# Routed experts in 47 blocks of 128 rows of one expert, in place of 40 blocks of two 64-row halves

## The reference

```python
# per token row t of the 8 * 128 = 1024 rows (hidden size 256)
scores = softmax(t @ gate_w.T)                 # 16 experts
top 4 experts of the row, weights scaled
routed = sum over the 4: w * (silu(g) * u) @ w2[e].T,  g, u = split(t @ w13[e].T)   # 176 wide
shared = sigmoid(t @ sgate_w.T) * ((silu(t @ Sg) * (t @ Su)) @ Sd)                  # 704 wide
out = x2 + routed + shared
```

## Time and profile before

| | |
|---|---|
| three runs | 398.63, 402.02, 402.61 us, median 402.02 |
| the profiled execution | 403.16 us, of which the span from the first to the last instruction is 401.3 us |
| busy in the span | PE 344.7 us (86%), DVE 227.7, ACT 207.2, POOL 178.8 |
| mean granted TensorE clock | 0.933 of full |
| moved by DMA | 72.54 MB, 181 GB/s over the span |

### The profile page before, as it was taken

One profiled execution on the slowest core, in us unless ns is written; L12 is line 12 of the kernel. 1 busy time (PEld: TensorE's weight loads), 2 busy tenths in 40 slices (PEclk: granted clock), 3 DMA queues, 4 the chain that ended last, 5 costly groups with the idle time before them and its releaser, 6 DMA issues.

```text
span 401.3 us, 7934 instructions
## 1 busy us (share of the span) xinstructions
PE 344.7 (86%) x2362; PEld 217.5 (54%) x2378; DVE 227.7 (57%) x688; ACT 207.2 (52%) x557; POOL 178.8 (45%) x212
## 2 busy tenths in 40 slices
PE   6988899999999978789996697897796888789893
PEld 2446576766777755477774343443443444346672
DVE  3387689889896899533725233333243333343884
ACT  1265688788897568344331354454344444552221
POOL 5481315343360516670664344655465455443000
PEclk9899899999999999758996599999899899999998
DMA  7997995979889452120682325554454455452931
GB/s 222 302 282 223 426 278 154 275 224 274 224 222 271 130 159 80 43 109 29 254 331 72 116 86 155 159 154 154 125 182 138 144 159 154 136 164 91 361 111 53
DMA packets 41747, 72.54 MB, mean 181 GB/s; under 512 B 5346, under 2 KB 29042, under 8 KB 40562
## 3 DMA queue, kind: packets, MB, share of 16 engines
q1 hardware_dynamic: 35490, 56.08, 46.5%
q0 software_dynamic: 5376, 15.13, 11.2%
q10 hardware_dynamic: 848, 0.92, 0.9%
HBM read 40.58 MB, written 31.53 MB: 180 GB/s over the span
## 4 chain that ended last, share of the span: by engine, by line
PE 40%; DVE 20%; issue 13%; ACT 10%; another core or an unknown queue 7%; POOL 5%; DMA 4%; ACTq 0%; DVEq 0%; POOLq 0%; SPq 0%
PE bank L1719 10%; ACT probs L656 6%; PE bank L1459 6%; PE bank L1741 5%; DVE neg_max L917 5%; PE bank L1731 3%; DVE probs_t L923 2%; PE bank L1381 2%; PE bank L1373 2%; PE bank L1429 2%; PE bank L1402 2%; PE bank L1604 1%; POOL y_picks L603 1%; PE bank L1709 1%
## 5 line engine op out<-in xcount | busy, mean ns | idle before, releaser
L1719 PE MATMUL bank<-w,xbt 128*64 x160 | 58.0, 489 | 20.4 <-ACT xbt L787 15.5
L656 ACT ACTIVATE probs<-bank,neg_max 128x128 f32<-128x128 f32 x256 | 69.9, 416 | 6.2 <-DVE neg_max L917 5.1
L603 POOL DMA_INDIRECT y_picks<-yb,ids x40 | 39.3, 982 | 51.9 <-DVE yb L1265 44.7
L1721 PE MATMUL bank<-w_odd,xbt 128*64 128x352 f32 x160 | 58.1, 489 | 0.0
L1258 DVE TENSOR_TENSOR hb<-sg,bank 128x176 f32<-128x176 f32 x40 | 13.5, 338 | 71.5 <-ACT sg L795 29.3
L611 POOL DMA_INDIRECT xb<-x_slots,rows x40 | 38.5, 962 | 21.8 <-DVE ids L1274 8.7
L1719 PEld LDWEIGHTS bank<-w,xbt 128*64 128x64 f32 x160 | 21.8, 144 | 44.6 <-issue 37.5
L795 ACT ACTIVATE sg<-bank 128x176 f32<-128x176 f32 x40 | 12.7, 317 | 63.8 <-PE bank L1721 43.0
L543 POOL DMA_INDIRECT x_slots<-x,slots x32 | 32.3, 1009 | 27.5 <-DVE slots L1046 19.5
L917 DVE TENSOR_REDUCE neg_max<-bank 128x4 f32<-128x512 f32 x64 | 41.5, 683 | 5.3 <-PE bank L1373 4.6
L1743 PE MATMUL bank<-w_odd,hbt 128*64 128x256 f32 x160 | 43.8, 398 | 0.0
(11 more groups left out here) (181 smaller groups left out, 740.5 us busy)
## 6 DMA issues: line engine op xcount, KB each, us to landing
x_slots<-zero_b SPq DMA_DIRECT2D x16, 1072.0 KB, 11.1
w_odd<-w_in_dram SPq DMA_DIRECT2D x40, 256.0 KB
w<-w_in_dram SPq DMA_DIRECT2D x4, 1408.0 KB, 12.0
w<-w_in_dram SPq DMA_DIRECT2D x4, 1024.0 KB
yg<-y_picks SPq DMA_DIRECT2D x8, 512.0 KB, 7.0
ktc<-keys_d SPq DMA_DIRECT2D x16, 192.0 KB
sw_raw<-shared_in_dram SPq DMA_DIRECT2D x6, 384.0 KB, 3.4
keys_d<-ctxt_h SPq DMA_DIRECT2D x4, 512.0 KB, 6.8
```

Of the source, the lines that this page charges most:

```text
L603: pool.indirect_dma_start(y_picks[:, :], bass.IndirectOffsetOnAxis(ids[:, n:n + 1], 0), yb[:, n % RB, :], None).then_inc(yb_placed[n % RB] ...
L656: ins = act.activation(probs[:, g, j, :], ps_s[g][:, 128 * j:128 * j + 128], ACT.Exp, bias=neg_max[:, g, j:j + 1])
L1719: pe.matmul(ps_gu[n % 2][0:ROWS, 0:GU], xbt[:, n % 2, k, 0:ROWS], w13[:, bass.ds(experts[n], 1), k, :].rearrange("p e n -> p (e n)"), star ...
L1721: ins = pe.matmul(ps_gu[n % 2][ROWS:128, 0:GU], xbt[:, n % 2, k, ROWS:128], w13_odd[:, n % 2, k, :], start=k == 0, stop=k == KC - 1)
```

## The change

The block is now 128 rows of one expert. With that bound there can be 47 blocks: (4096 + 16 * 127) // 128. One up weight and one down weight serve the whole block, so `copy_up`, `w13_odd` and `w2_odd` go, and so does the load of all down weights ahead; SP brings each block's down weights (`load_down`) and, as the rows of a block are adjacent in `x_slots`, its rows too (`load_rows`), each behind a register load. POOL keeps `place_rows` only. AHEAD = 2: the up product of chunks 6 and 7 and their element-wise steps stand ahead of the blocks. TensorE loads its packed words one at a time, seven of the eight inside the loop; ACT loads none.

```diff
-ROWS = 64
-NBLK = -(-((B * T * TOPK + NE * (ROWS - 1)) // ROWS) // 2)
-RW = 3
+NBLK = (B * T * TOPK + NE * 127) // 128
+AHEAD = 2
...
-        w13_odd = place("w13_odd", [128, 2, KC, GU])
-        w2_odd = place("w2_odd", [128, RW, KC, D])
-        w2 = place("w2", [128, NE, KC, D])
+        w2 = place("w2", [128, RB, KC, D])
...
+            def load_rows(n):
+                if n >= RB:
+                    sp.wait_ge(xbt_psum, n - RB + 1)
+                    sp.wait_ge(ids_ready, n - RB + 1)
+                row = sp.value_load(table[0:1, NBLK + n:NBLK + n + 1], min_val=0, max_val=EMPTY)
+                sp.dma_start(xb[:, n % RB, :], x_slots[bass.ds(row, 128), :]).then_inc(xb_loaded[n % RB], 16)
             def load_down(n):
-                if n >= RW:
-                    sp.wait_ge(yb_psum, n - RW + 1)
+                if n >= RB:
+                    sp.wait_ge(yb_psum, n - RB + 1)
                 e = sp.value_load(table[0:1, n:n + 1], min_val=0, max_val=NE - 1)
-                sp.dma_start(w2_odd[:, n % RW, :, :]...
+                sp.dma_start(w2[:, n % RB, :, :]...
             sp.wait_ge(x3_ready, B)
-            for i in range(4):
-                es = slice(4 * i, 4 * i + 4)
-                sp.dma_start(w2[:, es, :, :], w2_in[:, es, :, :]).then_inc(w2_loaded, 16)
             sp.wait_ge(table_ready, 3)
+            for n in range(RB - 1):
+                load_down(n)
+            sp.wait_ge(scattered, 16 * TOPK * B)
+            for n in range(RB + 1):
+                load_rows(n)
             for n in range(NBLK):
-                load_down(n)
+                if n + RB + 1 < NBLK:
+                    load_rows(n + RB + 1)
+                if n + RB - 1 < NBLK:
+                    load_down(n + RB - 1)
...
 # POOL: gather_rows goes, place_rows(n) for each block stays
 # ACT: copy_up goes
             take_y(0)
+            high_hidden(SC)
+            gate(SC + 1)
+            high_hidden(SC + 1)
...
-            gate(SC)
-            for n in range(SC, 2 * SC):
-                high_hidden(n)
-                if n + 1 < 2 * SC:
-                    gate(n + 1)
+            for n in range(SC + AHEAD, 2 * SC):
+                gate(n)
+                high_hidden(n)
...
 # DVE: block_table makes first rows and expert numbers on one partition
+            gated(SC)
             finish(0)
+            low_hidden(SC)
+            gated(SC + 1)
             for pair in range(2):
                 add_shared(0, pair)
+            low_hidden(SC + 1)
...
-            gated(SC)
-            for n in range(SC, 2 * SC):
+            for n, more in zip(range(SC + AHEAD, 2 * SC), (6, 6, 6, 0)):
+                gated(n)
                 low_hidden(n)
-                if n + 1 < 2 * SC:
-                    gated(n + 1)
-                combine(5 * (n - SC), min(5 * (n - SC) + 5, 3 * B))
+                combine(done, done + more)
+                done += more
+            combine(done, done + 3)
             finish(1)
+            combine(done + 3, 3 * B)
...
 # TensorE
             block_table()
+            rows_of(SC)
             down(5)
-            pe.wait_ge(table_ready, 2)
+            rows_of(SC + 1)
+            pe.wait_ge(table_ready, 3)
             for pair in range(2):
                 turn_rows(0, pair)
-            packed = [pe.value_load(...) for i in range(WORDS)]
+            load_word()
...
                 for k in range(KC):
-                    pe.matmul(ps_gu[n % 2][0:ROWS, 0:GU], xbt[:, n % 2, k, 0:ROWS], w13[expert n], ...)
-                    ins = pe.matmul(ps_gu[n % 2][ROWS:128, 0:GU], xbt[:, n % 2, k, ROWS:128], w13_odd[:, n % 2, k, :], ...)
+                    ins = pe.matmul(ps_gu[n % 2][:, 0:GU], xbt[:, n % 2, k, :], w13[expert n], ...)
...
                 for k in range(KC):
-                    pe.matmul(ps_yb[n % 2][0:ROWS, 0:D], hbt[:, n % 2, k, 0:ROWS], w2[expert n], ...)
-                    ins = pe.matmul(ps_yb[n % 2][ROWS:128, 0:D], hbt[:, n % 2, k, ROWS:128], w2_odd[:, n % RW, k, :], ...)
+                    ins = pe.matmul(ps_yb[n % 2][:, 0:D], hbt[:, n % 2, k, :], w2[:, n % RB, k, :], ...)
...
             for n in range(NBLK):
                 if n + 1 < NBLK:
                     block_up(n + 1)
+                if n % (PACK - 1) == 0:
+                    load_word()
...
             for n in range(SC, 2 * SC):
-                if n + 1 < 2 * SC:
-                    rows_of(n + 1)
                 down(n)
+                if n + AHEAD < 2 * SC:
+                    rows_of(n + AHEAD)
```

More of the change, by code:

```diff
@@ L96, in decoder_layer @@
         tri = place("tri", [128, 2, 128], BF16)
[L97 to L100, removed]
+        upto = place("upto", [NE, NE + 128 + NBLK])
+        dump = place("dump", [128, NBLK])
         of_block = place("of_block", [128, NBLK])
@@ L135, in decoder_layer @@
         counts_i = place("counts_i", [NE, 2], I32)
-        after = place("after", [NE, 2, 2 * NEXP])
-        table = place("table", [1, NBLK], I32)
-        words = place("words", [1, 2 * WORDS], I32)
+        after = place("after", [NE, NBLK])
+        table = place("table", [1, 2 * NBLK], I32)
+        words = place("words", [1, WORDS], I32)
         ex = place("ex", [128, B, NE])
@@ L604, in place_rows @@
                                         yb[:, n % RB, :], None).then_inc(yb_placed[n % RB], 16)
[L606 to L618, removed]
-            for n in range(NBLK):
[L620 to L624, removed]
+            for n in range(NBLK):
+                place_rows(n)
         @block.scalar
@@ L1572, in block_table @@
             def block_table():
-                pe.wait_ge(after_ready, 2)
-                for part in range(2):
-                    at = TABLE_AT + NBLK * part
-                    for i in range(2):
-                        pe.matmul(ps_t[ROWS * i:ROWS * i + ROWS, at:at + NBLK], upto[:, NE:NE + ROWS],
-                                  after[:, part, i:2 * NBLK:2], start=True, stop=True)
-                at = TABLE_AT + 2 * NBLK
-                for i in range(2):
-                    ins = pe.matmul(ps_t[0:1, at + NEXP * i:at + NEXP * i + NEXP], upto[:, NE:NE + 1], after[:, 0, i::2],
-                                    start=True, stop=True)
-                ins.then_inc(table_psum, 1)
+                pe.wait_ge(after_ready, 1)
+                pe.matmul(ps_t[:, TABLE_AT:TABLE_AT + NBLK], upto[:, NE:NE + 128], after[:, :], start=True, stop=True)
+                pe.matmul(ps_t[0:1, TABLE_AT + NBLK:TABLE_AT + 2 * NBLK], counts[:, 1:2], after[:, :], start=True, stop=True
+                          ).then_inc(table_psum, 1)
             def rows_of(n):
@@ L1684, in _, with load_word @@
             block_table()
+            rows_of(SC)
             down(5)
-            pe.wait_ge(table_ready, 2)
+            rows_of(SC + 1)
+            pe.wait_ge(table_ready, 3)
             for pair in range(2):
                 turn_rows(0, pair)
-            packed = [pe.value_load(words[0:1, i:i + 1], min_val=0, max_val=NE ** PACK - 1) for i in range(WORDS)]
+            packed = []
+            def load_word():
+                w = len(packed)
+                if w < WORDS:
+                    packed.append(pe.value_load(words[0:1, w:w + 1], min_val=0, max_val=NE ** PACK - 1))
             experts = {}
```

103 lines of the change are left out of this document (38 added, 65 removed).

## The result

| | before | after |
|---|---|---|
| median of four runs, us | 400.3 (398.0 to 402.6) | 377.5 (374.5 to 379.1) |
| ratio, 95% interval | | 0.942 (0.933 to 0.952) |
| profiled execution, its span | 403.16, 401.3 | 374.54, 372.7 |
| mean granted clock | 0.933 | 0.970 |

The account below looks back on a forecast made before the run. TensorE's order was taken to bound the blocks, with 25.7 us lost to stops. Start 227.0 + periods 122.8 + words 1.0 + stops 9.1 + last up to last down 4.9 + behind 31.2 = 396.0 us span; median 397, range 387 to 412.

Parts of the forecast that it names:

- The period: TensorE's time per block without a stop: unchanged at 2.79 us, 44 of them 122.8 us.
- The stops: TensorE's pauses in the blocks: 9.2 left, falling with its instructions, at half of 1.98 us each, 9.1 us in all.
- no stops: Rival for the blocks: stops came with paired matmuls, gathers or the copy, all gone; 388 us, chance 0.20.
- by block: Upper end of the full-stops rival (chance 0.28): late signals keep their length for each block, 30.5 us, time 418.
- The start: Third block's up at 227.0 in place of 232.94, as without the 4 MB load the ranks' signal comes near 207.
- The words: TensorE's loads of packed words inside the block loop: between 0 and 4.5 us, taken as 1.0.
- SP: SP's loads and issues: 2.3 us a block, hidden below 2.79; as a rival 3.15 us, time 407, chance 0.09.
- Behind the blocks: Stretch after the blocks, with DVE as the limit: 31.2 us in place of 34.6.
- the allowance: 0.3 us for links, added to the sum of 30.9 us for the stretch behind the blocks.

Follow-up runs that it names:

- e10_up_pairs: Changed kernel with only the up product made again as two 64-row matmuls, down product 128 rows wide; 390.5 us, ratio 0.982 to the kernel before.
- e1_pairs: Changed kernel with up and down products each made again as two 64-row matmuls side by side; 391.3 us, ratio 0.984 to the kernel before.
- e5_gather: Changed kernel with POOL's gather of 128 rows added for each block, into an unused buffer; 417.5 us, ratio 1.059 to the kernel before.
- e6_copy: Changed kernel with ACT's copy of 128 x 704 elements added for each block, behind the copy of the rows; 378.6 us, ratio 0.963 to the kernel before.
- e8_before_sp_rows: Kernel before with POOL's gathers replaced by SP's plain transfers of 128 adjacent rows, pairs and copy kept; 374.5 us, ratio 0.953 to the kernel before.
- e0_after_again: Changed kernel run once more, unaltered, beside other runs; 380.7 us, ratio 0.954 to the kernel before.
- e12_gather_half: Changed kernel with POOL's gather of 128 rows added for every second block only; 389.7 us, ratio 0.985 to the kernel before.
- e3_gather_copy: Changed kernel with POOL's gather and ACT's copy, ahead of the copy of the rows, both added for each block; 408.3 us, ratio 1.028 to the kernel before.

## Why the prediction was wrong

**The period (122.8 us, measured 110).** "A block up is four starts 0.29 us apart", and the wide groups showed the same pace: right, they are 0.30. "Downs are 256 columns before and after, transposes are unchanged. So the period stays 2.79": this is the first step that failed, by 12.8 us. I priced the instructions by their own pace and not the joints between them. A sum of the paces would have shown it: 4 up starts of 0.29, 4 transposes of 0.11 and 4 down starts of 0.22 are 2.48, and the period was 2.79; the timeline had joints of 0.40 and 0.32 where 0.29 and 0.22 were due. The price of seven more blocks was real, 7 x 2.50 = 17.5 us, but 40 x 0.29 = 11.6 came off the others. The rule of the Trainium skill on changes of mode, quoted with e10_up_pairs, spoke for this change, and I did not weigh it.

**The stops (9.1 us, measured 0).** The rival "no stops" named the gathers among three suspects and had 0.20; the forecast let the stops go with TensorE's instructions, and this is the second step that failed. What makes a stop is a row of indirect transfers on POOL, and the changed kernel has none before its last three placements. Neither instructions nor pairs nor the copy nor bytes had a part in it: e1_pairs has 40 matmuls and weight loads a block and no stop, e5_gather has 24 and 20 stops, e6_copy has the copy and no stop, and e8_before_sp_rows moves the same bytes for each block as the kernel before without one. (I counted 13 stops; the timeline has 15 periods of 3.9 us and more. The forecast is not touched, as only their total of 25.7 us enters it.) The clue was in rows I had: POOL's gather and placement each take 0.96 us and follow 0.3 us apart, 2.52 us for a period of 2.79, and the longest late signal, the ranks', lay in a row of scatters like it. I took the DMA share of 0.95 for its cause because it was the more striking number of the same stretch. The case "by block", 418, is out too. I had it stand if the stops were not fetches, as if they then had to stay the same for each block; that was a step of mine and not of the page. The packets of 16 KB still come, 15 of them, and no stop comes with them. That fetches are mostly hidden, as the Trainium skill says (Runtime: NRT & Kernel Launch, Instruction fetch mechanics), agrees with that.

**The start (227.0, measured 224.26).** The number was near by luck, the reason was wrong. The ranks' signal did not come at 207 for lack of the 4 MB load; it was 5.4 us late again, and the first scatter of batch 7 stands at 207.84 because this execution was 4.3 us ahead at the ranks. From the ranks on, the profiled executions of the changed kernel gain 0.4 us (e0_after_again) and 4.4 us (the first one), against the 5.9 I had, and the difference between the two is mostly the clock of the moved up products (0.6 us of it is a later signal of the ranks). In the working, 3.67 less 0.96 is 2.71 and not 2.5, which is 0.2 us.

**The words (1.0).** 111.05 - 44 x 2.50 = 1.05 us: right in size; in e0_after_again the same difference is 0.4.

**SP.** 1.10 us for each load and issue, from 216.22 to 217.32, so 2.2 a block, hidden: right, and by less than I thought, as the period is 2.50.

**Behind the blocks (31.2, measured 32.99).** DVE was the limit, as said. It waits 1.4 us for the last down product, which came late and at half clock, and the picks came 8.3 us behind the blocks (348.05) and not 7.6; of these 2.1 us the allowance took 0.3. In e0_after_again, with that product at full clock, the wait is 0.5 us, but the picks come 9.0 us behind the blocks, and the stretch is 32.8.

## What to carry to other kernels

Price the joints of a TensorE stream, not only its instructions: where 64-column and 128-column weights alternate, add 0.14 us for each change. Keep GpSimd's indirect transfers from following each other three or more in a row (pauses of 0.55 to 0.80 us in the kernel before, and one of 0.99 in e5_gather, did not end such a row) while another engine waits for TensorE, and give a plain transfer from another queue the part of them that is contiguous. A wait with no visible cause is found by laying the timelines of all engines side by side at its end, not by the largest number of the stretch.

## What was not expected of the hardware

- TensorE's completion is seen late by ACT and DVE while GpSimd issues indirect transfers 0.30 us apart. In a row of ten the ranks are seen 4.5 to 6.0 us behind their first matmul (0.4 with no row); in rows of six a signal is up to 4.2 us late, in rows of four up to 2.9, and in rows of three of e12_gather_half 0.5 to 1.2. Single transfers (the changed kernel) and the pairs of e3_gather_copy and e12_gather_half hold nothing back; in the kernel before, three down products were seen 0.5 to 0.7 us late at a pair. The long waits end near the end of the row, at the latest 1.5 us behind it, if the pause of 0.99 us in e5_gather is counted as inside a row. What holds the signal back no run shows. ACT's signals to DVE come through in 0.03 us in the same rows.
- A change between half-width and full-width weights costs 0.14 us at full clock.
- The same program had half the clock for 10 us ahead of the blocks in one profiled execution and full clock in another, in both behind an idle time of TensorE (3.1 and 2.5 us).
